# A two-layer transformer in one kernel: merged lookup copies, low weight parts in their own buffer, three input buffers, X loaded per batch, and GpSimd adding layer zero's down output

## What is computed

```
x = _layernorm(x + attention0(x, Wq, Wk, Wv, Wo))         # 32 query heads of 8, 8 key heads, softmax over 256 keys
x = _layernorm(x + ffn0(x))                               # 256 -> 768 -> 256
x = _layernorm(x + attention1(x, wq, wk, wv, wo))         # 16 query heads of 16, 8 key heads
x = _layernorm(x + ffn1(x))                               # 256 -> 688 -> 256

ffn0:  q(w) = w.astype(float8_e4m3fn);  g = silu((x @ q(gate_w)) * gate_scale)
       y = ((g * ((x @ q(up_w)) * up_scale)) @ q(down_w)) * down_scale
ffn1:  w = lut[idx] for gate, up and down (a table of 16 values);  y = (silu(x @ gate.T) * (x @ up.T)) @ down.T
```

## Time and profile before

| | us |
|---|---|
| median of 3 runs | 377.01 (376.22 to 380.54) |
| the profiled execution, its own time | 378.62 |
| its span, first to last instruction | 376.8 |
| PE busy | 314.0 |
| DVE busy | 286.6 |
| ACT busy | 218.2 |
| POOL busy | 160.5 |

### The profile page before, as it was taken

How to read it: one execution, slowest core, us unless ns; L and a number is a source line. 1 busy time by engine, 2 the same in 40 slices (tenths; PEclk the granted TensorE clock), 3 DMA queues, 4 the chain that set the end, 5 groups by cost and what they waited for, 6 DMA issues and landing times.

```text
span 376.8 us, 7304 instructions
## 1 busy us (share of the span) xinstructions
PE 314.0 (83%) x2592; PEld 197.7 (52%) x2592; DVE 286.6 (76%) x510; ACT 218.2 (58%) x391; POOL 160.5 (43%) x245
## 2 busy tenths in 40 slices
PE   4738337687878988989899899999979999999992
PEld 3524102132425563655447465765645678969992
DVE  7527999998889978888898798889868773445461
ACT  1644486888575737557666765675735576432340
POOL 4352371607046127342755628433912321543563
PEclk9965655859899989999999999999989999999998
DMA  7874520203201000040102200220136000000000
GB/s 210 275 191 108 153 84 32 82 21 95 57 30 27 1 27 23 2 119 10 50 3 86 66 3 24 66 63 2 53 110 250 2 3 1 18 14 30 2 30 28
DMA packets 23492, 23.08 MB, mean 61 GB/s; under 512 B 3348, under 2 KB 23316, under 8 KB 23328
## 3 DMA queue, kind: packets, MB, share of 16 engines
q1 hardware_dynamic: 23312, 20.40, 18.8%
q10 hardware_dynamic: 144, 2.21, 1.6%
HBM read 10.47 MB, written 3.26 MB: 36 GB/s over the span
## 4 chain that ended last, share of the span: by engine, by line
PE 53%; DVE 15%; ACT 10%; issue 9%; SPq 5%; POOL 4%; DMA 3%; DVEq 0%; POOLq 0%; ACTq 0%
PE FB L1105 12%; ACT PB L694 7%; PE FB L1116 7%; PE PV L1049 7%; PE MM L994 5%; DVE MX L815 5%; PE SC L1024 4%; PE FB L1077 4%; PE FB L950 3%; PE SC L1029 3%; PE FB L968 2%; DVE LV L921 2%; SPq L471 2%; PE FB L973 2%; SPq L478 2%
## 5 line engine op out<-in xcount | busy, mean ns | idle before, releaser
L815 DVE TENSOR_REDUCE MX<-MM 128x4 f32<-128x1024 f32 x96 | 117.1, 1220 | 27.7 <-PE MM L994 21.6
L694 ACT ACTIVATE PB<-SC 128x1024 f32<-128x1024 f32 x96 | 98.1, 1022 | 50.2 <-PE SC L1024 25.9
L994 PE MATMUL MM<-KS,QS 62*128 62x256 bf16 (+1 forms) x384 | 48.6, 299 | 26.5 <-DVE MX L815 20.0
L602 POOL TENSOR_SCALAR LV<-LB,LD,LT 128x432 f32<-128x432 f32 x80 | 56.9, 726 | 21.3 <-ACT LB L738 20.8
L1049 PE MATMUL PV<-PB,VP 128*32 128x256 f32 x768 | 63.2, 410 | 0.2 <-ACT PB L694 0.2
L584 POOL TENSOR_TENSOR HL<-HF,HH 128x256 fp32r<-128x256 f32 (+1 forms) x48 | 35.0, 733 | 66.0 <-ACT HH L670 65.7
L1105 PE MATMUL FB<-XH,W 128*128 128x256 f32 x288 | 54.4, 297 | 0.3 <-DVE QR L792 0.3
L994 PEld LDWEIGHTS MM<-KS,QS 62*128 62x128 bf16 (+1 forms) x384 | 18.8, 98 | 58.7 <-DVE MX L815 35.7
L921 DVE COPY_PREDICATED LV<-LB,LV 128x432 f32<-128x432 uint8 x70 | 43.1, 676 | 4.1 <-POOL LV L602 4.0
L1105 PEld LDWEIGHTS FB<-XH,W 128*128 128x128 f32 x288 | 41.0, 189 | 8.7 <-issue 6.9
L1105 PE MATMUL FB<-XL,W 128*128 128x256 f32 x192 | 38.4, 281 | 0.0
(11 more groups left out here) (81 smaller groups left out, 463.3 us busy)
## 6 DMA issues: line engine op xcount, KB each, us to landing
QS<-QP SPq DMA_DIRECT2D x48, 128.0 KB, 2.4
IX<-in_idx SPq DMA_DIRECT2D x10, 216.0 KB, 2.9
dw<-LO SPq DMA_DIRECT2D x10, 216.0 KB, 2.1
W<-dw ACTq DMA_DIRECT2D x1, 2160.0 KB, 8.8
KS<-KP SPq DMA_DIRECT2D x24, 64.0 KB, 2.0
XT<-in_xt SPq DMA_DIRECT2D x4, 256.0 KB, 3.3
X<-in_x SPq DMA_DIRECT2D x1, 1024.0 KB, 7.2
out<-X SPq DMA_DIRECT2D x4, 256.0 KB, 2.1
```

The source lines that it names most:

```text
L602: ins = pool.tensor_scalar(LV[:, i, :], LB0[:, :], LD[:, i:i + 1], LT[:, 2 * i:2 * i + 1], ALU.mult, ALU.add)
L694: act.activation(PB[:, quad % PB_QUADS, kt, :, :], SC[:, :, :], ACT.Exp, scale=DH[layer(j)] ** -0.5).then_inc(exp_done, 1)
L815: dve.tensor_reduce(mx, MM[:, :, :].rearrange("p (f i) s -> p f i s", f=2), axis=AX.X, op=ALU.max).then_inc(max_red, 1)
L994: ins = pe.matmul(MM[:, 2 * f + i, :], QS[lo:lo + r, j % NST, qs + h, qt * P:(qt + 1) * P], keys(j)[lo:lo + r, j % NST, ks, :], start=True ...
```

## The change

Six things are changed in the code, and the five strings of ORDER are written anew.

1. `lut2`, `lut3` and `lut4` are one COPY_PREDICATED each, over 4, 2 and 1 blocks of 432 columns, with the mask broadcast.
2. The low parts have a buffer of their own, W1L, which takes the place of LV and IX. `reload` is now ten transfers of 216 KB from SP; it waits for dw alone. The first seven release `gu.4.0`, the last three `down.4.0`.
3. XT has three buffers.
4. X is loaded in four transfers, one a batch, ahead of other loads, each with a semaphore of its own.
5. Layer zero's `down`: ACT copies the bank into DN (the RAW buffers, free by then), POOL multiplies by DS and adds to X (`dsum`), and DVE only takes the statistics.
6. Q8A and Q8B lie in AA, which frees their room.

```diff
-                    for i in range(0, LUT // 2, 2 * gap):
-                        ins = dve.copy_predicated(LV[:, i, :], LB[:, k, :], LV[:, i + gap, :])
-                    link(ins)
+                    n = LUT // 4 // gap
+                    link(dve.copy_predicated(LV[:, 0:LUT // 2:2 * gap, :], LB[:, k:k + 1, :].broadcast_to((P, n, LUT_W)),
+                                             LV[:, gap:LUT // 2:2 * gap, :]))
...
+                elif kind == "dsum":
+                    j = step[1]
+                    b = batch(j)
+                    pool.wait_ge(dn_in, b + 1)
+                    if b == 0:
+                        pool.wait_ge(ld_wo, 16 * 2)
+                    dn = DN.rearrange("p (t d) -> p t d", t=TT)
+                    link(pool.tensor_tensor(dn, dn, DS[:, :].rearrange("p (o d) -> p o d", o=1).broadcast_to((P, TT, D)),
+                                            ALU.mult))
+                    pool.tensor_tensor(X[:, b, :, :], X[:, b, :, :], dn, ALU.add).then_inc(x_sum, 1)
...
+                elif kind == "down":
+                    j = step[1]
+                    act.wait_ge(down_ready, j + 1)
+                    if batch(j) >= 1:
+                        act.wait_ge(x_sum, batch(j))
+                    act.activation(DN, bank[:, :], ACT.Copy).then_inc(dn_in, 1)
...
-                    dve.wait_ge(down_ready, j + 1)
                     if layer(j) == 0:
-                        for t in range(TT):
-                            ins = dve.tensor_tensor(bank[:, t * D:(t + 1) * D], bank[:, t * D:(t + 1) * D],
-                                                    DS[:, :], ALU.mult)
-                        link(ins)
-                    dve.tensor_tensor(x2, bank[:, :], x2, ALU.add).then_inc(fill_free[slot], 1)
-                    wait_free(dve, step)
+                        dve.wait_ge(x_sum, b + 1)
...
+                elif kind == "reload":
+
+                    c = step[1]
+                    sp.wait_ge(dw_wr, 16 * N_LUT)
+                    at = slice(c * LUT_W, (c + 1) * LUT_W)
+                    sp.dma_start(W1L[:, at].bitcast(F32), dw[:, at]).then_inc(low_in[c >= N_LUT_GU], 16)
...
-                    if j >= 2:
-                        sp.wait_ge(q_ready, j - 1)
-                        sp.wait_ge(kv_ready, j - 1)
+                    if j >= NXT:
+                        sp.wait_ge(q_ready, j - NXT + 1)
+                        sp.wait_ge(kv_ready, j - NXT + 1)
...
+        "qstack.6.2 mt.5.1 lutlow.9 qstack.7.0 mt.6.0 reload.0 reload.1 qstack.7.1 kstack.7.0 qstack.7.2 kstack.7.1 "
+        "kstack.7.2 reload.2 reload.3 reload.4 reload.5 reload.6 reload.7 reload.8 reload.9 mt.6.1 mt.7.0 mt.7.1 "
```

More of the change, by code:

```diff
@@ L45, with batch, earlier, later @@
 W1_COLS = N_LUT * LUT_W
+N_LUT_GU = -(-2 * DT * I1 // LUT_W)
+SEQ = ((0, 0), (0, 1), (0, 2), (0, 3), (1, 0), (1, 1), (1, 2), (1, 3))
+NXT = 3
 def layer(j):
-    return j // B
+    return SEQ[j][0]
+def batch(j):
+    return SEQ[j][1]
+def earlier(j):
+    return SEQ.index((0, batch(j)))
+def later(j):
+    return SEQ.index((1, batch(j)))
+def first(l):
+    return min(j for j in range(JOBS) if layer(j) == l)
 def halves(j):
@@ L287, in two_layer_kernel @@
         LB0 = sb("LB0", [P, LUT_W])
-        LV = sb("LV", [P, 8, LUT_W])
+        spare = ExitStack()
+        LV = spare.enter_context(nc.sbuf_tensor("LV", [P, 8, LUT_W], F32))
+        IX = spare.enter_context(nc.sbuf_tensor("IX", [P, 2, LUT_W], I32))
+        spare.close()
+        W1L = sb("W1L", [P, W1_COLS], F32R)
         LT = sb("LT", [P, LUT])
@@ L312, in two_layer_kernel @@
         dw = nc.dram_tensor("dw", (P, W1_COLS), F32, kind="Internal").ap()
-        ld_xt = [sem(f"ld_xt{i}") for i in range(2)]
+        ld_xt = [sem(f"ld_xt{i}") for i in range(NXT)]
         ld_w0 = sem("ld_w0")
@@ L318, in two_layer_kernel @@
         ld_s = sem("ld_s")
-        ld_x = sem("ld_x")
+        ld_wo = sem("ld_wo")
+        ld_x = [sem(f"ld_x{b}") for b in range(B)]
         ld_raw = [sem(f"ld_raw{i}") for i in range(2)]
@@ L371, in two_layer_kernel @@
         dw_wr = sem("dw_wr")
-        low_in = sem("low_in")
+        low_in = [sem(f"low_in{i}") for i in range(2)]
         ib_done = sem("ib_done")
@@ L392, in stack_count, with xt_count @@
             return 16 * NPROD * (j // NST + 1)
+        def xt_count(j):
+            return 16 * sum(layer(i) == 0 for i in range(j % NXT, j + 1, NXT))
         def rows_count(n):
@@ L515, in _ @@
                                      MP[16 * half:16 * half + 16, n % 2, :]).then_inc(m_rows[n % 2], 16)
+                elif kind == "ldx":
+                    b = step[1]
+                    sp.dma_start(X[:, b, :, :], x[b].rearrange("(t p) d -> p t d", p=P)).then_inc(ld_x[b], 16)
                 elif kind == "ldq8":
@@ L529, in _ @@
                     sp.wait_ge(x_new, norms["down", j] + 1)
-                    sp.dma_start(out[j - B].rearrange("(t p) d -> p t d", p=P),
-                                 X[:, j - B, :, :]).then_inc(out_wr, 16)
+                    sp.dma_start(out[batch(j)].rearrange("(t p) d -> p t d", p=P),
+                                 X[:, batch(j), :, :]).then_inc(out_wr, 16)
             sp.wait_ge(out_wr, 16 * B)
@@ L610, in _ @@
                 kind = step[0]
-                if kind in ("q", "kv", "mt", "back", "tr", "gu"):
+                if kind in ("q", "kv", "mt", "back", "tr", "gu", "down"):
                     slot = fill[step][0]
@@ L624, in _ @@
                     act.wait_ge(kv_ready, j + 1)
-                    if j in (0, B):
-                        act.wait_ge(ones_pool, 1 if j == 0 else 2)
+                    if j == first(l):
+                        act.wait_ge(ones_pool, l + 1)
                     if j >= NST:
@@ L656, in _ @@
                     _, j, w = step
-                    act.wait_ge(tr_ready[w], j + 1)
+                    act.wait_ge(tr_ready[w], (j if w == 0 else batch(j)) + 1)
                     if w == 0:
@@ L1012, in _ @@
                         pe.wait_ge(m_rows[m % 2], rows_count(m))
-                    if v == 0 and j == B:
+                    if v == 0 and j == first(1):
                         pe.wait_ge(ones_in, 16 * 2)
@@ L1112, in _ @@
                     pe.wait_ge(h_parts, 6 * j + i + 1)
+                    if l == 1 and i == 0:
+                        pe.wait_ge(low_in[1], 16 * (N_LUT - N_LUT_GU))
                     products = ((0, HH), (0, HL), (1, HH))[:2 + l]
```

78 lines of the change are left out of this document (42 added, 36 removed), and 229 rows, old and new, of the table ORDER.

## The result

| | us (median) | ratio to before, 95% interval |
|---|---|---|
| before | 377.12 (376.22 to 380.54, 4 runs) | |
| changed | 388.02 (387.43 to 388.73, 4 runs) | 1.0273 [1.0206, 1.034] |

What follows compares the result with a forecast made beforehand. DVE was taken to set the pace from 28 to 100 us, with PE and DVE both near full to 280 and PE full after; -3.0 - 1.4 - 3.6 + 1.0 = -7.0 us gave 370.0 us, range 358 to 379.

Steps and rivals of the forecast that it cites:

- the down path: Layer zero's down output, from PE's last `down` through POOL's sum to the transpose: +1.0 us, bounds 0 and 7.6.
- `tr.2.1` alone late behind POOL: Expected sign in the new profile: of the transposes behind the down output, only job 2's would wait for POOL.
- five or more: Scores PE was said to have between `down.0`, `down.1` or `down.3` and their transposes; only four behind `down.2`.
- What freed DVE time is worth: DVE time saved by merged copies and the moved down sum: -1.4 us from 54 to 100 us, -3.6 from 100 to 280.
- The share of 0.45: From 100 to 280 us, DVE's part of PE's waiting, applied to 8.1 us of freed DVE time: -3.6 us.
- The start: Regrouped first transfers: first reduction at about 27.3 us, `mt.0.0` at 46.4; -3.0 us, bounds -4.5 and 0.
- Merged copies: Lookup pieces on DVE: three copies instead of seven, 40 starts less at 0.10 us, 4.0 us of DVE saved.
- The reading of 1 ns: Lookup copies on DVE: about 1 ns a column, from 592 more columns taking 0.58 us.
- Rival C: Merged lookup copies take 2 ns a column instead of 1: 393 us; slower than 380.8, this above all, had 0.09.
- The reloads at 0: Low parts' transfers ahead of `mt.6.1` on SP: taken as 0 us, bounds 0 and +7.0.
- rival B: Gain given back as `mt.6.1` waits behind reloads or POOL's sum is late: 376.6 to 377.0 us; with small mixtures 0.21.
- A new order that leaves PE idle where I haven't looked: Named among what would make the forecast wrong, as something rows of before can't show; no size given.

Runs made afterwards that it cites:

- i: Changed kernel with only the transposes behind the attention output (`tr.j.0`) reading a loaded WO, so not waiting for GpSimd; values differ: 380.49 us, 7.5 less.
- j: Changed kernel with only the transposes behind layer zero's down output (`tr.j.1`) reading a loaded WO, so not waiting for GpSimd; values differ: 384.67 us, 3.3 less.
- e: Kernel before with merged lookup copies alone: 377.19 us, ratio 0.999 to before.
- a: Changed kernel's code with the order of before and the down output left on DVE: 375.21 us, ratio 0.9938 to before.
- k: Changed kernel with five lookup copies moved in DVE's order from just ahead of the statistics of jobs 0, 2 and 3 to behind them: 387.14 us.
- l: Changed kernel with the first two reload transfers moved behind job 7's last key stack transfer on SP: 390.34 us, ratio 1.0338 to before.
- b: Changed kernel, new order kept, with layer zero's down output scaled and added on DVE again: 397.83 us, ratio 1.0543 to before.
- h: Order of before on the changed code, with the down sum on GpSimd and DVE's statistics one to three steps later: 385.75 us, ratio 1.0175.
- f: Changed kernel with PE's transposes behind a normalisation reading a loaded WO, so not waiting for GpSimd; values differ: 377.82 us, ratio 0.9996 to before.
- m: Changed kernel with six of the eight layer zero transposes one or two scores later in PE's, ACT's and DVE's orders: 388.09 us, ratio 1.0266.

## Why the prediction was wrong

- **The step that failed** is the one that lets the new order cost nothing but the down path: "I take +1.0 us; bounds 0 and 7.6", with "`tr.2.1` alone late behind POOL". Only the four transposes behind the down output were looked at. All eight wait in the trace, 10.5 us, and those behind the attention output carry 6.4 of them and 7.5 us of the time (i). The order would have told: between `wo.j.1` and `tr.j.0` PE had 4, 4, 3 and 1 scores before and 3, 3, 2 and 2 after, and in DVE's list a copy of 2.1 us stands right behind `wo.3`, with two more ahead of `tr.3.0`. The scores alone wouldn't have told it for `tr.3.0`, which gained one and waits longest; there the copies held GpSimd up by 2.5 us (1.92 us for 0.19 at 242.52, 1.91 for 1.09 at 245.58). Nor did the forecast have a price for what a stop does to the granted clock; by the estimate above it is about 1.7 us for each of the three long ones. Against the old order, with the down output on DVE and otherwise the same code, the change loses 12.8 us (388.02 against 375.21).
- **The size of the down path.** 4.3 us instead of 3.4 to the statistics and 8.2 instead of 7.2 in all; `tr.2.1` waited 2.19 us where 1.0 was forecast; the four of them cost 3.3 us (j), inside the bounds. The cover was misread too: behind the last `down` part PE has 4, 5, 4 and 3 scores ahead of the four transposes, not "five or more" for three of them. POOL came to 177.6 us, 6.6 above the forecast 171: the additions took 2.1 us instead of 1.27 each (3.4 in all), and normalisation was slowed too.
- **What freed DVE time is worth**: -1.4 and -3.6 us were forecast, and no gain is seen. DVE's work fell by 8.3 us (forecast about 9.6), but from 54 to 100 us it stood idle for 10.2 of 46 us, where it had been busy for 42.5: less work on an engine that waits gave nothing. e shows the same alone: 3.0 us less of copies, no change. The share of 0.45 was not a measurement, and for the copies in the old order it is near zero.
- **The start** came out right by luck: `mt.0.0` at 46.60 for 46.4. The first reduction was 1.7 us earlier than forecast (25.63 for 27.3), and from there to `mt.0.0` it took 21.0 us for 19.1, no less than before (20.8): DVE's named waits in it add up to 3.2 us, nearly all for ACT, where 1.6 was allowed. 1.56 us of the 2.84 were lost again ahead of the first exponential, and the sum carried the 3.0 us to the end. The old order on the changed code has that exponential as early (a), so the new lists brought nothing there.
- **Merged copies**: 3.3 us of DVE for 4.0, form at 1.2 ns a column. The reading of 1 ns came from comparing a reduction with a copy. Rival C (a slow form, 393 us) ended near the time, but by another mechanism: its copy of 1728 columns took 2.08 us undisturbed, far from the 3.5 that it needs. Of it only the two engines' holding each other up was there, and k gained nothing by moving the copies away.
- **The reloads at 0** were right to within about 1 us; the mechanism of rival B is real (l: 2.87 us) and lies just outside the place that was chosen.
- "A new order that leaves PE idle where I haven't looked" had been named among what would make it wrong; that is what happened, and it was given no chance of its own and no place in the range.

**What stays open.** The order and the down sum can't be priced apart. With the down output on DVE the old order takes 375.2 us (a) and the new one 397.8 (b); with it on GpSimd 385.8 (h) and 388.0. So in the old order moving the sum costs 10.5 us and in the new one taking it back costs 9.8, and the new order alone costs 22.6 or 2.3, by where the sum is. Shown is that the chain from DVE's addition over GpSimd's normalisation to PE's transpose carries about 10 us in the new order against 3 to 6 in the old one; in f's profile it came back more as busy time than as idle time (7.3 and 4.6 us). Not shown is how much of that is GpSimd's being held up and how much the shorter distances. Not shown is one place to mend: copies away and transposes later gave 0.9 and 0 us, both together lost 9, and moving the reloads lost 2.3 and 5.3. Why m and k together cost 9 us was read from two waits and not tried further.

## What to carry to other kernels

When a change rewrites the order, count for every dependence across engines (not only the ones that the change touches) what stands between producer and consumer before and after: a place that lost one or two steps is a term of the sum. Work taken from an engine that waits was worth nothing here, so price a saving by who waits there, and keep an order's chance of costing apart from the code's: here the code was worth -0.6% and the order with the down sum +3.4%. The wait that a profile names can be emptied without gaining anything; only removing the dependence (f, i, j) told what it carries. Compare busy time as well as idle time, since a stop of PE can be paid again in the clock behind it.
